# Expert down products two blocks behind, a fourth slot for inner activations, two places for spare blocks, and a second attention turned by DMA

## The chip, the cores and the metric

The kernel runs on one core of one Trainium2 chip. The metric is the time of one execution on the device in microseconds (us). Engines by their short names: PE (TensorE, PEld its weight loads), DVE (VectorE), ACT (ScalarE), POOL (GpSimd), SP (SyncE); SPq, POOLq are the parts of SP and POOL that issue DMAs.

## The reference

Four sequences of 512 tokens, width 512. First a cross attention, then a mixture of eight experts (two per token) beside a shared feed-forward net:

```python
x = x + xattn(layernorm(x), ctx, Wq, bq, Wk, bk)
    # q = ctx Wq^T + bq, k = ctx Wk^T + bk, A = softmax(q k^T)
    # x_m[l, m] = sum_n layernorm(x)[l, n] * A[m, n]
h = layernorm(x)
x = x + moe(h) + (silu(h @ sw_gate) * (h @ sw_up)) @ sw_down * sigmoid(h @ shared_gate_w)
    # moe: softmax over 8 logits, the two largest, made to sum to 1;
    # expert e: (silu(h @ w_gate[e]) * (h @ w_up[e])) @ w_down[e],
    # w_gate, w_up: 512 x 352, w_down: 352 x 512; shared net: 512 x 1408, 1408 x 512
```

## The kernel before, in words

Every large product is made of three products of 16-bit halves (a high and a low part, `PAIRS`), so that each product of two matrices is three matmuls, and whoever makes an operand makes both halves: usually ACT the high one (a cast) and DVE the low one (a subtraction).

**Stage 1, the prologue (0 to about 48 us).** Attention of sequence b=0 and the start of that of b=1, with the order on each engine written out by hand. On DVE: statistics, normalize, five small operations that split the router's weights (`gw3`), then row maxima and scaling of the attention rows in turn.

**Stage 2, the shared net (to about 445 us).** `ffn_block(t)` for t = 0 to 3, 11 tiles j of 128 inner units each: PE does gate(j), up(j) and down(j-2), twelve matmuls each. Between them it does pieces of the attention of b = t+1. Tables (`AT_POINT_FIRST` for t=0, `AT_POINT`, `AT_POINT_LAST`) say at which point (j, "gate"/"up"/"down") which piece stands, and all engines read the same tables, so a piece stands at the same point of each engine's own program. The pieces: `attn`/`attn_lows` (attention rows transposed by PE, halved by ACT and DVE), `attn_high`/`attn_low` with `turn_attention` (rows halved first, then transposed by DMA from SP's queue; used for b = 2 and 3), `mix` (the product with normed x, 48 matmuls), `assign`/`places` (places of tokens in the experts' lists), `stats2`, `norm2`, `halves`. The shared net's weights are loaded and split tile by tile meanwhile, tiles 0 to 3 by POOL.

**Stage 3, the experts (445 us to the end).** Rows were scattered by expert into a scratch tensor `xs_dram`. 39 blocks of 128 rows are worked through: as many as any routing could fill. The reference sends 529, 574, 526, 500, 502, 468, 474 and 523 rows of these inputs to the eight experts, which is 5+5+5+4+4+4+4+5 = 36 real blocks (0 to 35); blocks 36 to 38 are spare, and all their rows lead to padding rows of `out`. For a block k: SP's `load_block` brings x transposed, PE does gate and up (12 matmuls of 352 columns each), ACT `block_silu`, DVE `block_product`, ACT `hidden_high` and DVE `hidden_low` make halves, SP's `turn_hidden` transposes them by DMA into one of three slots, PE does `expert_down` (9 matmuls), ACT `weigh` scales the result into `yblk`, and POOL `add_result` adds it to `out` by an indirect DMA. PE's order is up(k), gate(k+1), down(k-1). Block 38's inner activations are turned by PE itself (`turn_last_hidden`), then halved (`last_hidden_high`, `last_hidden_low`).

Adds of blocks that may hit the same rows must not overlap. Block k always waits for the add of block k-2; it waits for that of block k-1 too, unless `table[3]` says that both have the same expert (whose rows are all different). For spare blocks `same_expert` is 0, so each waits for the one before:

```python
                if k >= 2:
                    pool.wait_ge(y_added[k % 2], 16 * (k // 2))
                ...
                if k >= 1:
                    pool.wait_ge(y_added[(k - 1) % 2], ahead)
```

Of the kernel before, what the change touches and what calls it, by code (L numbers as in the profile page):

```python
# [13 lines left out]
P = 128  # L14
# [89 lines left out]
def build_xattn_moe(nc, x, ctx_in, w_q, b_q, w_k, b_k, gate_w, w_gate, w_up, w_down,  # L104
# [23 lines left out]
    X_SLOTS = 4  # L128
    XF = E + 4
    SPARE = E * NT  # L130
    DUMP = SPARE + (NBLK - MIN_BLK) * P
    META = H
# [38 lines left out]
    with ExitStack() as stack:  # L171
# [12 lines left out]
        def four_banks(b, stage):  # L184
            return first_two(b) and (b == 0 or stage != "logits") and stage != "assign"
# [45 lines left out]

        attn_rows = normed_own.rearrange("p t h -> p (t h)").bitcast(F16).rearrange("p (t n) -> p t n", t=RT)

        class AttentionPlace:

            def __init__(self, ctx_rows, normed, xnT, expo, attn_space):
                self.ctx_rows, self.normed, self.xnT, self.expo = ctx_rows, normed, xnT, expo
                self.attnT = attn_space.rearrange("p (a t n) -> p a t n", a=2, t=RT)

# [16 lines left out]
        def place(b):  # L256
# [6 lines left out]
        hidT = hidden[:, :, :, :].rearrange("p s a n -> p (s a n)")[:, 0:3 * 2 * DC * P].rearrange(  # L263
            "p (s a n) -> p s a n", s=3, a=2)
        hid_rows = hT[:, 1].rearrange("p a c s -> p (a c s)").bitcast(BF16)[:, 0:3 * 2 * DC * P].rearrange(
            "p (s a n) -> p s a n", s=3, a=2)
# [61 lines left out]
        pad_id = sb("pad_id", [P, 1], I32)  # L328
        count = sb("count", [P, E], F32)
# [13 lines left out]
        same_expert = sb("same_expert", [P, NBLK], F32)  # L343
        pad_full = sb("pad_full", [P, E], F32)
# [56 lines left out]
        aT_in = [sem(f"aT_in{b}") for b in range(2, B)]  # L401
# [5 lines left out]
        hid_in = [sem(f"hid_in{i}") for i in range(3)]  # L407
# [20 lines left out]
        def _(sp):  # L428
# [48 lines left out]
            sp.dma_start(place(1).ctx_rows, ctx_in[1].rearrange("(t p) c -> p t c", p=P)).then_inc(ctx1_loaded, 16)  # L477
            load_rows(1, x1_loaded)
# [18 lines left out]
            def turn_attention(b):  # L497

                sp.wait_ge(energy_done, RT * b + RT)
                for i in range(RT):  # L500
                    sp.wait_ge(a_row_low, RT * (b - 2) + i + 1)
                    sp.dma_start(by_tile(place(b).attnT, i), attn_rows[:, i, :],
                                 transpose=True).then_inc(aT_in[b - 2], 16)
# [11 lines left out]
            for j in range(2, 8):  # L515
                load_unit_tile(j)
# [1219 lines left out]
```

## Time and profile before

| | us |
|---|---|
| median of 3 runs (lowest, highest) | 683.58 (683.12, 683.95) |
| the profiled execution's own time | 683.55 |
| its span in the profile | 681.8 |
| PE busy in it | 653.4 (96%) |
| DVE, ACT, POOL busy | 301.3, 229.1, 163.6 |

The profile is of one execution, and its time lies within the runs. A row of the timeline begins with the start and the length in us; in square brackets stands how long the engine had been idle and what ended that. Line numbers are those of the kernel before.

### The profile page before, as it was taken

What the parts mean: (1) busy time and instruction counts of PE and PEld (TensorE: products, weight loads), DVE (VectorE), ACT (ScalarE), POOL (GpSimd) and SP (SyncE); (2) the same over time, 40 slices, a digit from 0 to 9 for tenths busy, and PEclk for the clock granted to TensorE, in tenths of its full rate; (3) what the DMA queues carried; (4) which work ended last, traced back from release to release, by engine and by line L of the source; (5) the groups of instructions that cost most, each with busy time, mean ns of one, the idle gap of its engine ahead of it and who ended that gap; (6) DMA issues with size and microseconds to landing.
All of it is one profiled execution on the core that took longest, in us unless ns stands there. A gap on an engine that the chain in (4) does not pass through costs nothing.

```text
span 681.8 us, 10320 instructions
## 1 busy us (share of the span) xinstructions
PE 653.4 (96%) x3426; PEld 333.1 (49%) x3426; DVE 301.3 (44%) x703; ACT 229.1 (34%) x341; POOL 163.6 (24%) x134
## 2 busy tenths in 40 slices
PE   8889999999999999999999999999999999999990
PEld 5454444444444444444444444455555555555550
DVE  3998574525523445432549874452222222222220
ACT  3445143313620223630434543432222322222320
POOL 2560180004000004100344360013222222222221
PEclk9989999999999999999999999999999999999996
DMA  8531097313430313430167886447879888878962
GB/s 278 186 92 48 1 304 211 114 58 131 95 61 0 57 37 125 125 63 0 31 169 250 309 302 173 141 118 129 131 128 132 132 131 133 135 126 139 131 74 31
DMA packets 146899, 85.77 MB, mean 126 GB/s; under 512 B 109721, under 2 KB 131481, under 8 KB 146850
## 3 DMA queue, kind: packets, MB, share of 16 engines
q1 hardware_dynamic: 134722, 56.25, 35.6%
q0 software_dynamic: 10544, 27.30, 18.2%
q10 hardware_dynamic: 1584, 1.57, 0.7%
q8 instruction: 31, 0.51, 0.3%
q14 instruction: 18, 0.15, 0.1%
HBM read 32.76 MB, written 27.29 MB: 88 GB/s over the span
## 4 chain that ended last, share of the span: by engine, by line
PE 75%; DVE 8%; DMA 8%; SPq 2%; issue 2%; ACT 1%; POOL 1%; POOLq 0%; ACTq 0%
PE bank L1594 27%; PE bank L1642 16%; PE bank L1609 14%; PE bank L1669 9%; PE bank L1451 5%; DMA hidden<-hT 3%; DMA out<-staging,token_blk 2%; DMA staging<-L_ffn_w_gate 2%; PE bank L1408 1%; SPq L531 1%; DMA arena<-x 1%; PE bank L1417 1%; POOL arena L641 1%; DVE arena L1288 1%; DVE stats L936 1%
## 5 line engine op out<-in xcount | busy, mean ns | idle before, releaser
L1594 PE MATMUL bank<-hT,arena 128*128 128x512 f16 x1056 | 237.7, 379 | 0.5 <-DVE prod L1314 0.5
L1594 PEld LDWEIGHTS bank<-hT,arena 128*128 128x128 bf16 x1056 | 102.6, 98 | 126.2 <-issue 4.6
L1642 PE MATMUL bank<-arena,hx_odd 128*128 x936 | 145.9, 313 | 0.0
L1609 PE MATMUL bank<-arena,hidden 128*128 128x512 bf16 x528 | 120.4, 379 | 0.0
L1642 PEld LDWEIGHTS bank<-arena,hx_odd 128*128 128x128 f16 x936 | 90.8, 97 | 54.0 <-issue 0.9
L657 POOL DMA_INDIRECT out<-staging,token_blk x39 | 61.1, 1566 | 163.5 <-ACT staging L913 133.1
L1351 DVE TENSOR_TENSOR prod<-silu_sb,bank 128x352 f32<-128x352 f32 x39 | 20.3, 521 | 149.8 <-PE bank L1642 149.8
L1669 PE MATMUL bank<-arena,hidden 128*128 (+1 forms) x351 | 82.3, 379 | 3.5 <-DMA hidden<-hT 1.7
L1609 PEld LDWEIGHTS bank<-arena,hidden 128*128 128x128 bf16 x528 | 51.3, 98 | 63.1 <-issue 2.3
L1314 DVE TENSOR_TENSOR prod<-silu_sb,bank 128x512 f32<-128x512 f32 x44 | 30.1, 685 | 73.8 <-PE bank L1594 69.7
L875 ACT ACTIVATE silu_sb<-bank 128x512 f32<-128x512 f32 x44 | 26.2, 595 | 104.4 <-PE bank L1594 104.2
L869 ACT CAST hidden<-prod 128x512 bf16<-128x512 f32 x44 | 26.9, 617 | 86.3 <-DVE prod L1314 86.3
L1669 PEld LDWEIGHTS bank<-arena,hidden 128*128 128x128 bf16 (+1 forms) x351 | 34.2, 98 | 41.0 <-issue 6.1
L913 ACT ACTIVATE staging<-bank,w_blk 128x512 f32<-128x512 f32 x39 | 26.8, 687 | 63.8 <-PE bank L1669 63.8
L1319 DVE TENSOR_TENSOR hidden<-prod,hidden 128x512 bf16<-128x512 f32 x44 | 35.0, 799 | 29.1 <-ACT hidden L869 28.9
L609 POOL TENSOR_TENSOR rstd<-var_eps,minus_half 128x4 f32<-128x4 f32 x8 | 9.7, 1207 | 156.5 <-DVE var_eps L949 156.3
L1451 PE MATMUL bank<-arena 128*128 128x512 f16 x192 | 43.1, 379 | 0.0
L901 ACT CAST hT<-prod 128x352 bf16<-128x352 f32 x38 | 18.4, 484 | 63.5 <-DVE prod L1351 63.5
L1288 DVE TENSOR_TENSOR arena<-staging,arena 128x1408 bf16<-128x1408 f32 (+1 forms) x14 | 23.5, 1679 | 14.8 <-ACT arena L845 14.8
L1451 PEld LDWEIGHTS bank<-arena 128*128 128x128 f16 x192 | 18.8, 98 | 23.0 <-issue 0.6
L845 ACT CAST arena<-staging 128x1408 bf16<-128x1408 f32 (+1 forms) x18 | 25.1, 1398 | 13.4 <-DMA staging<-L_ffn_w_gate 9.9
L892 ACT ACTIVATE silu_sb<-bank 128x352 f32<-128x352 f32 x39 | 18.1, 463 | 28.8 <-PE bank L1642 28.8
(190 smaller groups left out, 512.8 us busy)
## 6 DMA issues: line engine op xcount, KB each, us to landing
staging<-L_ffn_w_gate SPq DMA_DIRECT2D x6, 704.0 KB, 5.2
staging<-L_ffn_w_up SPq DMA_DIRECT2D x6, 704.0 KB, 5.9
arena<-x SPq DMA_DIRECT2D x3, 1024.0 KB, 7.4
out<-arena POOLq DMA_DIRECT2D x3, 1024.0 KB, 4.8
staging<-L_ffn_w_down SPq DMA_DIRECT2D x6, 512.0 KB, 4.8
staging<-L_ffn_sw_gate SPq DMA_DIRECT2D x11, 256.0 KB, 3.1
staging<-L_ffn_sw_up SPq DMA_DIRECT2D x11, 256.0 KB, 3.7
staging<-L_ffn_sw_down SPq DMA_DIRECT2D x11, 256.0 KB, 4.6
```

The lines of the kernel that those rows point to most:

```text
L657: nc.gpsimd.indirect_dma_start(out=out[:, :], out_offset=bass.IndirectOffsetOnAxis(ap=token_blk[:, k:k + 1], axis=0), in_=yblk[:, k % 2, : ...
L869: nc.scalar.copy(hidden[:, j % 3, HI, :], prod[:, j % 2, :]).then_inc(hid_hi, 1)
L875: nc.scalar.activation(silu_sb[:, :], gate_ps[:, :], ACT.Silu).then_inc(silu_ready, 1)
L913: nc.scalar.activation(yblk[:, k % 2, :], bank[4 + k % 2][:, :], ACT.Copy, scale=w_blk[:, k:k + 1]).then_inc(y_ready, 1)
L1288: nc.vector.tensor_tensor(arena[:, at + gap:at + gap + n], piece_space[piece_slot(q)][:, 0:n], arena[:, at:at + n], ALU.subtract).then_inc ...
L1314: nc.vector.tensor_tensor(prod[:, j % 2, :], silu_sb[:, :], up_ps[:, :], ALU.mult).then_inc(prod_ready, 1)
L1319: nc.vector.tensor_tensor(hidden[:, j % 3, LO, :], prod[:, j % 2, :], hidden[:, j % 3, HI, :], ALU.subtract).then_inc(hid_lo, 1)
L1451: op = nc.tensor.matmul(att_bank(b, "mix", i)[:, :], place(b).xnT[:, xp, c, i * P:(i + 1) * P], place(b).attnT[:, ap, c, :], start=(c == 0 ...
L1594: op = nc.tensor.matmul(ps[:, :], weights[:, j, wp, kind, c * P:(c + 1) * P], hT[:, t % 2, hp, c, :], start=(c == 0 and s == 0), stop=(c = ...
L1609: op = nc.tensor.matmul(out_ps[i][:, :], hidden[:, j % 3, hp, i * P:(i + 1) * P], weights[:, j, wp, DOWN, :], start=(j == 0 and s == 0), s ...
L1642: op = nc.tensor.matmul(ps[:, 0:I], xT[:, k % X_SLOTS, xp * KC + c, :], arena[:, bass.ds(at + (part_at(0, part) + wp * low_gap(part) + c * ...
L1669: op = nc.tensor.matmul(ps[:, :], hidT[0:n, k % 3, hp, c * P:(c + 1) * P], arena[0:n, bass.ds(at + (DOWN_AT + wp * DN + c * H), H)], start ...
```

## The change

Six edits, all in the order of work or in what waits for what; the results are computed with the same products.

1. PE's order in the expert stage becomes up(k), gate(k+1), down(k-2); inner activations have four slots (`HID_SLOTS`), and ACT's `weigh` follows by one block more. At the end PE transposes the last block's activations inside down(37), ahead of its last three matmuls.
2. Spare blocks go alternately to two sets of padding rows; `same_place` lets a spare block whose predecessor is spare skip the wait for it. Three more small DMAs fill the odd spare blocks' token columns, and one more clears the second padding rows.
3. The attention of b=1 is turned as those of 2 and 3 are: halves by ACT and DVE, four DMA transposes on SP's queue, no PE transposes.
4. `mix` of b=1 and what follows from it stand one tile j later; it uses two banks instead of four, so that down(0) of t=0 no longer waits for it.
5. In the prologue DVE takes row maxima and scaling ahead of the five `gw3` operations, and one row maximum ahead of normalize.
6. SP holds the load of x[1] (and all behind it) until x[0] has landed; POOL splits tile 3 after `h_low` instead of after normalize; SP loads tile 8 ahead of `turn_h(1)`.

```diff
 AT_POINT_FIRST = {
-    (1, "gate"): [("attn_lows", 0)],
-    (1, "up"): [("attn", 0), ("attn", 1), ("attn", 2), ("attn", 3)],
-    (1, "down"): [("assign", 0)],
-    (2, "gate"): [("mix", 0), ("mix", 1), ("mix", 2), ("mix", 3)],
-    (2, "up"): [("stats2", 0)],
+    (1, "gate"): [("attn_high", 0), ("attn_high", 1)],
+    (1, "up"): [("attn_low", 0), ("attn_low", 1), ("attn_high", 2), ("attn_high", 3)],
+    (1, "down"): [("attn_low", 2), ("attn_low", 3), ("assign", 0)],
     (2, "down"): [("halves_before", 0)],
-    (3, "gate"): [("norm2", 0)],
-    (3, "up"): [("halves", 0)],
+    (3, "gate"): [("mix", 0), ("mix", 1), ("mix", 2), ("mix", 3)],
+    (3, "up"): [("stats2", 0)],
+    (4, "gate"): [("norm2", 0)],
+    (4, "up"): [("halves", 0)],
...
+            sp.wait_ge(x0_loaded, 16)
             load_rows(1, x1_loaded)
...
-            for j in range(2, 8):
+            for j in range(2, 6):
+                load_unit_tile(j)
+            turn_attention(1)
+            for j in range(6, 9):
                 load_unit_tile(j)
             turn_h(1)
...
-                if k >= 3:
-                    sp.wait_ge(ed_done, k - 2)
+                if k >= HID_SLOTS:
+                    sp.wait_ge(ed_done, k + 1 - HID_SLOTS)
...
                 for n in range(NBLK - MIN_BLK):
-                    pool.dma_start(xs_dram[SPARE + n * P:SPARE + (n + 1) * P, :],
-                                   pad_row[:, :]).then_inc(spare_filled, 16)
+                    spare = xs_dram[SPARE + n * P:SPARE + (n + 1) * P, :]
+                    if n % 2:
+                        pool.dma_start(spare[:, 0:TOKEN], pad_row[:, 0:TOKEN]).then_inc(spare_filled, 16)
+                        pool.dma_start(spare[:, TOKEN:XW], pad_odd[:, :]).then_inc(spare_filled, 16)
+                    else:
+                        pool.dma_start(spare, pad_row[:, :]).then_inc(spare_filled, 16)
...
-            pool.wait_ge(normed_ready[1], RT)
+            pool.wait_ge(hlo_ready, KC)
             for j in range(3, POOL_TILES):
                 split_unit_tile(j)
...
             for k in range(NBLK - 1):
                 hidden_high(k)
                 block_silu(k + 1)
-                if k > 0:
-                    weigh(k - 1)
+                if k > 1:
+                    weigh(k - 2)
+            weigh(NBLK - 3)
+            last_hidden_high()
             weigh(NBLK - 2)
-            last_hidden_high()
             weigh(NBLK - 1)
...
+                    nc.vector.tensor_tensor(same_place[:, 1:NBLK], same_expert[:, 1:NBLK], ended[:, 0:NBLK - 1, E - 1],
+                                            ALU.add)
...
-                    nc.vector.scalar_tensor_tensor(out=table[:, 3, 1:NBLK], in0=same_expert[:, 1:NBLK], scalar=-16.0,
+                    nc.vector.scalar_tensor_tensor(out=table[:, 3, 1:NBLK], in0=same_place[:, 1:NBLK], scalar=-16.0,
...
+                if i < 2 and b == 1:
+                    pe.wait_ge((logits_read, places_read)[i], b)
+                if i >= 2 and b >= 1:
                     pe.wait_ge(added, RT * b + i - 1)
...
                         if t == 0:
-                            pe.wait_ge(added, RT * b + RT)
+                            pe.wait_ge(exp_done, RT * b + RT)
+                            pe.wait_ge(xlo_ready, KC * b + KC)
...
                     n = chunk(c)
+                    if k == NBLK - 2 and c == DC - 1:
+                        turn_last_hidden()
...
-                if k == 1:
+                if k == 2:
                     pe.wait_ge(piece_low_dve, PIECES - POOL_LOW)
-                if k > 0:
-                    expert_down(k - 1, down_from)
-                down_from = pe.value_load(table[0:1, 2, k:k + 1], min_val=0, max_val=(E - 1) * 2 * DN)
-            turn_last_hidden()
-            expert_down(NBLK - 1, down_from)
+                if k > 1:
+                    expert_down(k - 2, down_from.pop(0))
+                down_from.append(pe.value_load(table[0:1, 2, k:k + 1], min_val=0, max_val=(E - 1) * 2 * DN))
+            expert_down(NBLK - 2, down_from.pop(0))
+            expert_down(NBLK - 1, down_from.pop(0))
```

Where this moves instructions, at three places. First PE in `ffn_block(0)`, before: from up(0), gate(1) and up(1) on (the 36 matmuls of L1594; L1434 is `turn_attn`, L1498 to L1504 `places`, L1451 `mix`, L1609 down):

```order
L1594 MATMUL bank<-hT,arena 128x512 x36
L1434 MATMUL bank<-ident,hx_odd 128x128 x16
L1498 MATMUL bank<-mask,earlier 128x32
L1501 MATMUL bank<-mask,ones 128x24
L1501 MATMUL bank<-mask,ones 128x16
L1501 MATMUL bank<-mask,ones 128x8
L1504 MATMUL bank<-mask,ones 128x8 x4
L1594 MATMUL bank<-hT,arena 128x512 x12
L1451 MATMUL bank<-arena 128x512 x48
L1594 MATMUL bank<-hT,arena 128x512 x12
L1609 MATMUL bank<-arena,hidden 128x512 x12
```

The same place on PE after the change (L1613 gate and up, L1629 down, L1472 `mix`):

```order
L1613 MATMUL bank<-hT,arena 128x512 x36
L1519 MATMUL bank<-mask,earlier 128x32
L1522 MATMUL bank<-mask,ones 128x24
L1522 MATMUL bank<-mask,ones 128x16
L1522 MATMUL bank<-mask,ones 128x8
L1525 MATMUL bank<-mask,ones 128x8 x4
L1613 MATMUL bank<-hT,arena 128x512 x24
L1629 MATMUL bank<-arena,hidden 128x512 x12
L1613 MATMUL bank<-hT,arena 128x512 x12
L1472 MATMUL bank<-arena 128x512 x48
L1613 MATMUL bank<-hT,arena 128x512 x12
```

The 16 transposes are gone, and up(2), down(0) and gate(3), 36 matmuls, now stand ahead of `mix`.

Second, DVE in `ffn_block(0)` after the change, from the last `inverse_sum` of b=1 to the product of tile 2 (L979 `x_low`, L1331 a product, L1027 `attn_row_low`, L1336 `low_part`); before, four `attn_low` stood between `x_low` and the product, and none behind it:

```order
L994 RECIPROCAL inv_sum<-sum_scaled 128x1 [waits sum_ready]
L979 TENSOR_TENSOR arena<-bank,arena 128x512 [waits xhi_ready] x4
L1331 TENSOR_TENSOR prod<-silu_sb,bank 128x512 [waits silu_ready,up_done]
L1027 SCALAR_TENSOR_TENSOR arena<-hx_odd,inv_sum,arena 128x512 [waits a_row_high] x2
L1336 TENSOR_TENSOR hidden<-prod,hidden 128x512 [waits hid_hi] x2
L1027 SCALAR_TENSOR_TENSOR arena<-hx_odd,inv_sum,arena 128x512 [waits a_row_high] x2
```

The last two of these rows release the last two DMA transposes of `turn_attention(1)`.

Third, ACT at the end of the program, before, from `hidden_high` of block 37 on (L901; L892 `block_silu`, L913 `weigh`, L905 `last_hidden_high`):

```order
L901 CAST hT<-prod 128x352 [waits hid_in1,ep_ready]
L892 ACTIVATE silu_sb<-bank 128x352 [waits ep_ready,eg_done]
L913 ACTIVATE staging<-bank,w_blk 128x512 [waits y_added0,meta_ready,ed_done]
L913 ACTIVATE staging<-bank,w_blk 128x512 [waits y_added1,meta_ready,ed_done]
L905 CAST hidden<-bank 128x384 [waits last_turned]
L913 ACTIVATE staging<-bank,w_blk 128x512 [waits y_added0,meta_ready,ed_done]
```

And after (L918, L909, L930 and L922):

```order
L918 CAST hT<-prod 128x352 [waits hid_in1,ep_ready]
L909 ACTIVATE silu_sb<-bank 128x352 [waits ep_ready,eg_done]
L930 ACTIVATE staging<-bank,w_blk 128x512 [waits y_added1,meta_ready,ed_done]
L930 ACTIVATE staging<-bank,w_blk 128x512 [waits y_added0,meta_ready,ed_done]
L922 CAST hidden<-bank 128x384 [waits last_turned]
L930 ACTIVATE staging<-bank,w_blk 128x512 [waits y_added1,meta_ready,ed_done]
L930 ACTIVATE staging<-bank,w_blk 128x512 [waits y_added0,meta_ready,ed_done]
```

Behind the last silu four blocks are still to be weighed, 35 to 38, where there were three.

## Rows read from the trace of the kernel before

**Rows 1.** Stretches: length, busy us (instructions) of PE, PEld, DVE, ACT, POOL; PEclk, DMA share, GB/s.

```profile
45.00:48.00 3.00, 3.00 (x16) 2.98 (x15) 2.93 (x7) 1.92 (x5) 2.35 (x2) 0.50 0.51 146
68.00:85.00 17.00, 17.00 (x81) 7.67 (x79) 8.99 (x23) 3.12 (x4) 2.12 (x1) 1.00 0.00 1
```

**Rows 2.** Timeline, PE in `ffn_block(0)` around the second attention.

```profile
51.95 7.93 PE L1594 MATMUL bank<-hT,arena 128*128 128x512 f16 x36
60.97 2.36 PE L1434 MATMUL bank<-ident,hx_odd 128*128 128x128 f32 x16 [1.09 <-DVE arena L961]
...
65.95 10.52 PE L1451 MATMUL bank<-arena 128*128 128x512 f16 x48
76.31 2.75 PE L1594 MATMUL bank<-hT,arena 128*128 128x512 f16 x12
```

**Rows 3.** Timeline, PE in the expert stage: first products, first down, block 38's up.

```profile
445.22 9.11 PE L1642 MATMUL bank<-arena,hx_odd 128*128 x60
455.20 2.12 PE L1669 MATMUL bank<-arena,hidden 128*128 x9 [0.86 <-DMA hidden<-hT]
...
658.17 1.96 PE L1642 MATMUL bank<-arena,hx_odd 128*128 x12
```

**Rows 4.** Chain that ended last, two points four blocks apart: start, us, what.

```profile
513.72 3.58 PE bank L1642 x24
...
535.83 3.59 PE bank L1642 x24
```

**Rows 5.** Timeline, the end: adds of blocks 35, 36, 38, `weigh` of 36 and 38.

```profile
653.99 1.55 POOL L657 DMA_INDIRECT out<-staging,token_blk  x1 [4.15 <-ACT staging L913]
...
658.37 0.69 ACT L913 ACTIVATE staging<-bank,w_blk 128x512 f32<-128x512 f32 x1 [1.48 <-PE bank L1669]
659.33 1.56 POOL L657 DMA_INDIRECT out<-staging,token_blk  x1 [3.79 <-ACT staging L913]
...
666.05 0.69 ACT L913 ACTIVATE staging<-bank,w_blk 128x512 f32<-128x512 f32 x1 [2.89 <-PE bank L1669]
670.34 1.56 POOL L657 DMA_INDIRECT out<-staging,token_blk  x1 [3.88 <-DMA out<-staging,token_blk]
```

**Rows 6.** Timeline, DVE in `ffn_block(0)`: last inverse, `x_low`, two `low_part`.

```profile
59.35 0.15 DVE L973 TENSOR_SCALAR sum_scaled<-exp_sum 128x1 f32<-128x1 f32 x1
...
60.13 2.48 DVE L961 TENSOR_TENSOR arena<-bank,arena 128x512 f16<-128x512 f32 x4
...
65.52 1.46 DVE L1319 TENSOR_TENSOR hidden<-prod,hidden 128x512 bf16<-128x512 f32 x2
```

**Rows 7.** b=2's `attn_row_low` (timeline), and line L502's DMA transposes (ns; to landing).

```profile
185.36 1.41 DVE L1009 SCALAR_TENSOR_TENSOR arena<-arena,inv_sum 128x512 f16<-128x512 f32 x2
...
L502 SPq DMA_TRANSPOSE arena<-arena x8: 1232/1282/1338, 186.2 to 296.2; - x8
DMA to landing us min/median/max: 3.1/3.2/3.4
```

**Rows 8.** Timeline, prologue: energies of b=0, DVE's order, the product that waits.

```profile
13.79 3.60 PE L1417 MATMUL bank<-arena 128*128 128x512 f32 x8
14.70 1.92 DVE L955 TENSOR_SCALAR arena<-arena,mean_var,rstd 128x512 f32<-128x512 f32 x4 [1.17 <-POOL rstd L609]
...
17.53 1.28 DVE L966 TENSOR_REDUCE neg_max<-bank 128x1 f32<-128x512 f32 x2
...
22.61 0.68 DVE L961 TENSOR_TENSOR arena<-bank,arena 128x512 f16<-128x512 f32 x1
23.27 1.88 PE L1408 MATMUL bank<-arena 128*128 128x512 f32 x4
```

**Rows 9.** The adds of line L657 as a group: time to landing after issue.

```profile
DMA to landing us min/median/max: 4.6/4.8/6.8
```

**Rows 10.** Timeline, PE's idle time ahead of the slow stretch.

```profile
44.19 3.00 PE L1461 MATMUL bank<-ident,arena 128*128 128x128 f32 x16 [2.62 <-DVE arena L955]
```

**Rows 11.** Timeline, the issue of `turn_h(1)`'s four DMA transposes on SP.

```profile
96.62 11.29 SPq L512 DMA_TRANSPOSE hT<-hx_odd  x4
```

More of the change, by code:

```diff
@@ L128, in build_xattn_moe @@
     X_SLOTS = 4
+    HID_SLOTS = 4
     XF = E + 4
@@ L184, in four_banks @@
         def four_banks(b, stage):
-            return first_two(b) and (b == 0 or stage != "logits") and stage != "assign"
+            return first_two(b) and (b == 0 or stage not in ("logits", "mix")) and stage != "assign"
         def att_bank(b, stage, i):
@@ L400, in build_xattn_moe @@
         xT_in = [sem(f"xT_in{b}") for b in range(2, B)]
-        aT_in = [sem(f"aT_in{b}") for b in range(2, B)]
+        aT_in = [sem(f"aT_in{b}") for b in range(1, B)]
         hT_in = [sem(f"hT_in{b}") for b in range(1, B)]
@@ L406, in build_xattn_moe @@
         hid_pad, hid_row_high, hid_row_low = sem("hid_pad"), sem("hid_row_high"), sem("hid_row_low")
-        hid_in = [sem(f"hid_in{i}") for i in range(3)]
+        hid_in = [sem(f"hid_in{i}") for i in range(HID_SLOTS)]
         last_turned, last_high, last_low = sem("last_turned"), sem("last_high"), sem("last_low")
@@ L513, in turn_h @@
                                  transpose=True).then_inc(hT_in[b - 1], 16)
-            for j in range(2, 8):
+            for j in range(2, 6):
+                load_unit_tile(j)
+            turn_attention(1)
+            for j in range(6, 9):
                 load_unit_tile(j)
             turn_h(1)
-            for j in range(8, UT):
+            for j in range(9, UT):
                 load_unit_tile(j)
@@ L677, in _ @@
             fill_spare()
-            pool.dma_start(out[NT:NT + P, :], pad_row[:, 0:H]).then_inc(spare_filled, 16)
+            for n in range(2):
+                pool.dma_start(out[NT + n * P:NT + (n + 1) * P, :], pad_row[:, 0:H]).then_inc(spare_filled, 16)
             send_rows(0)
@@ L742, in attn_row_high @@
                 act.wait_ge(inv_ready, RT * b + n + 1)
-                if n == 0:
+                if n == 0 and b >= 2:
                     act.wait_ge(x_row_low, b - 1)
-                nc.scalar.activation(attn_rows[:, n, 0:S], place(b).expo[:, n, :], ACT.Copy,
+                elif n == 0:
+                    act.wait_ge(x_turned, KC * b + KC)
+                nc.scalar.activation(place(b).attn_rows[:, n, 0:S], place(b).expo[:, n, :], ACT.Copy,
                                      scale=inv_sum[:, n:n + 1]).then_inc(a_row_high, 1)
@@ L1181, in _ @@
             statistics(0, 0)
+            row_max(0, 0)
             normalize(0, 0)
+            row_max(0, 1)
+            scale_attn(0, 0)
+            row_max(0, 2)
+            scale_attn(0, 1)
+            row_max(0, 3)
+            scale_attn(0, 2)
+            x_low(0, 0)
             gw_ps = bank[7][:, 0:KC * NL].rearrange("p (k e) -> p k e", k=KC)
@@ L1253, in attention @@
                         attn_row_low(b, i)
-                    elif stage == "attn_lows":
-                        for c in range(KC):
-                            attn_low(b, c)
                     elif stage == "mix":
@@ L1563, in attention @@
                         energy(b, i)
-                    elif stage == "attn":
-                        turn_attn(b, i)
                     elif stage == "mix":
@@ L1725 @@
     n_tokens, n_experts = shape[0] * shape[1], inputs["L0_ffn_w_gate"].shape[0]
-    out = nc.dram_tensor("out", (n_tokens + P, shape[2]), F32, kind="ExternalOutput").ap()
+    out = nc.dram_tensor("out", (n_tokens + 2 * P, shape[2]), F32, kind="ExternalOutput").ap()
     xs_rows = n_experts * n_tokens + (n_experts - 1) * P + n_experts * P
```

97 lines of the change are left out of this document (47 added, 50 removed).

## The prediction

> **What bounds the kernel now.** I read the stretches first: PE is busy for all of 68 to 85 us at full clock [rows 1], and of the whole span 96% (the table). So only two kinds of time can be won: PE's own waits and work, and what follows PE's last matmul. I then followed PE alone for its waits, and the chain of waits for the end. Three places matter here.
>
> In the shared net PE waits 1.09 us ahead of the second attention's transposes and then spends 2.36 us on them [rows 2]; up(1) ended at 51.95 + 7.93 = 59.88, `mix` begins at 65.95 and takes 76.31 - 65.95 = 10.36 for 48 matmuls, so 2.59 for a group of twelve.
>
> In the expert stage an undisturbed block takes (535.83 - 513.72) / 4 = 5.53 us, 3.58 of it gate and up, 1.95 down [rows 4]. From the first product at 445.22 to block 38's up at 658.17 lie 212.95 us [rows 3]. They hold 77 half products (39 gates, 38 ups) and 37 downs, which is 36 x 5.53 + 5 x 1.79 + 1.95 = 210.0. So PE lost 3.0 us, and a row shows how: the first down waited 0.86 us idle for the DMA that transposes inner activations (`hidden<-hT`).
>
> At the end PE is not the bound. Block 38's `weigh` is over at 666.05 + 0.69 = 666.74, its add starts at 670.34, after a wait for a DMA: the add before it [rows 5]. The adds of 35, 36 and 38 start at 653.99, 659.33 and 670.34, so one waiting for the other costs 5.34, then 11.01 / 2 = 5.5 each.
>
> **Second attention.** Removed from PE: the wait and the transposes. I assume that gate(0) starts when it did (prologue, below). Then up(1) ends at 59.88, `places` takes at most some 0.4 (estimate: between 60.97 and the next gate, at 65.95 - 2.59 = 63.36, all but 0.03 us is the transposes, so it mostly overlaps), and gate(2), up(2), down(0), gate(3) run from 60.3 to 70.7. Will the operands be there? On DVE: inverse from 59.35, about 0.35; `x_low` 2.48 [rows 6] to 62.2; the product of tile 1, of `low_part`'s shape, 0.7, to 62.9, in time for up(2) at 62.9; two `attn_row_low` 1.4 [rows 7]; two `low_part` 1.46 to 65.7, the first of them in time for down(0) at 65.5; two more `attn_row_low` to 67.1. ACT's four casts run ahead of these, and its silu and halves have the 2.59 us of each PE group. SP issues the third transpose at 66.4 and the fourth at about 67.75; each takes 1.28 to issue and lands 3.2 later [rows 7]: 72.25. So `mix` starts at 72.35 and PE waits 1.65 us: a new stall in place of the old one. Up(2), down(0) and gate(3) (7.77 us) have moved ahead of it, so the start that compares with 65.95 is 72.35 - 7.77 = 64.6, whatever `places` takes. **Gain 1.4.** Bounds: with transposes that land by 70.7 it is 3.0; with the slowest landing of the row, 3.4, 1.2. What follows is one tile later, with 7.77 us per tile to cover it. `mix` in two banks makes its third part wait for the add of the first, which has the 2.59 us of the second part for its 0.7. SP's queue: tile 6 stands behind the transposes but waits for tile 4's split anyway, in tile 2's up; tile 8 is loaded ahead of `turn_h(1)`, which needs 11.3 us of SP and leaves 20 to the logits in tile 8.
>
> **Prologue.** DVE works nearly without a break from 14.70 on. Normalize started there; now the row maximum goes first, and the first energy is done at 13.79 + 3.60 / 4 + latency, about 14.85. The order behind it is the same work in another sequence. The `gw3` operations (16.6 to 17.5 [rows 8]) now come after the third scaling and one `x_low`; PE's project(1,1), which overwrites their bank and started at 23.27, waits for them. Summed, DVE reaches their end at 14.85 + 0.64 + 1.83 (to normalize's end) + 5.5 (three row maxima, scalings and `x_low`) + 1.0 = 23.8 at most, 23.2 if its present wait for ACT goes. I take nothing; bounds -0.6 and +0.3, since DVE is the chain there. Holding x[1] costs nothing by these rows: statistics of b=1 come after all this.
>
> **Down two behind.** The transpose of block k now has one more block, 5.53 us, to land in; the waits were a fraction of a microsecond each. SP's work per block does not grow, and the fourth slot keeps its wait for `ed_done` at a block long done. Adds, `yblk` slots and silu keep their distance to PE. **Gain 3.0**, bounds 2.0 (if a third of the loss is not the transposes') and 3.0.
>
> **The end.** Down(35) moves behind gate(38), where down(36) stood, so `weigh`(35) starts where that of 36 did (658.37) with one down less ahead of it: 1.95 earlier, and with the gains above. An add starts 1.0 after its `weigh` does (block 36) [rows 5]. Block 36 is spare but 35 is not, so 36 still waits for 35: +5.34. 37 has no wait for 36 any more. 38 goes to the same rows as 36 and waits for it: +5.5. In all 658.37 - 1.95 + 1.0 + 5.34 + 5.5 = 668.3 before the gains above, against 670.34: **gain 2.0**. So three of the four adds still follow each other; the change takes one landing out of the chain but puts one block more behind PE's last gate. Block 38's `weigh`, 666.74 less 4.4 = 662.3 even if the moved transposes win nothing, is ready before its add may start (668.3 - 4.4 = 663.9), so that move is hidden by 1.6 us. Bounds: an add's landing lies between 4.6 and 6.8 [rows 9]; if 37, issued meanwhile, delays 36's landing to the slowest, the gain is 0; if 35's add starts earlier than I think, 2.5.
>
> The four more DMAs on POOL stand ahead of its first row scatter, in the shared net; they delay that by four issues, and what waits for the scatter (ACT's halving of x for b=2, SP's first block load) comes tiles later. Nothing; without that cover, four issues.
>
> **Sum.** 1.4 + 3.0 + 2.0 = 6.4. The profiled execution took 683.55, next to the median 683.58: 683.55 - 6.4 = **677.1**.
>
> **Rivals.**
> - The clock. PE ran at 1.2 GHz from 45 to 48 (granted 0.50 [rows 1]), after 2.62 us without work [rows 10]. If the new wait before `mix` does the same, three microseconds at half rate cost 1.5: 678.6. Against it: the wait is shorter, between full groups, and the present wait of 1.09 was not followed by a fall (1.00 in 68 to 85). The Trainium skill ("TensorE: Matmul & The Clock Gate", "Why this matters for your kernels") warns of idle gaps between bursts of matmuls for just this reason; the trace agrees at 45 us and shows no fall for a short gap.
> - The stalls stay: the transposes were late by little, and something else (PE's own instruction supply) sets part of the loss. Two of the three microseconds stay: 679.1. For it: only 0.86 of the loss is a row here. Against: that row names the DMA.
> - The end gains nothing, as two adds in flight share the DMA engines and land late: 679.1.
> - Slower: the four transposes of the second attention issue as those of `turn_h(1)` did, 11.29 us for four [rows 11]. From 63.6 that ends at 74.9, lands at 78.1, PE waits 7.4 instead of 1.65, and after such a wait the clock falls, 1.5 more: 677.1 + 5.75 + 1.5 = 684.4. It decides from a landing past about 77.2 on (5.0 later, with the fall). Against: `turn_h(1)` ran beside POOL's row scatters, while in 68 to 85 the DMA engines are idle (share 0.00). The Trainium skill ("DMA: Bandwidth & Descriptors", "Issuing engines are not separate DMA queues") says that DMAs of all engines run on the same 16 and interleave; by that rule it is the other traffic that counts, and the row shows none here.
>
> **How the numbers follow.** Forecast 0.58; clock 0.12; stalls stay 0.10; end gains nothing 0.13; slower 0.05; nothing measurable 0.02 (several bounds at once). The range goes from 674.8 (transposes in time 1.6, end 0.5, prologue 0.3, taken from 677.1) to 680.6 (the end's and the clock's rivals together, 2.0 + 1.5): about 0.85. A measurement of this kernel can tell some 0.2% (1.4 us) from no change: faster 0.91, same 0.04, slower 0.05.
>
> **What would show it.** After: no PE transposes of the second attention, one wait of about 1.7 us before `mix` in tile 3; no wait for `hidden<-hT` in the expert stage, whose first product to block 38's up takes about 208 us (one down less); the last four adds with 36 some 5.3 after 35, 37 within 2 to 3 of 36, 38 some 5.5 after 36. The prediction is wrong if DVE's chain before 60 us moved by over half a microsecond, if the wait before `mix` exceeds 3, or if the add of 38 waits for its `weigh`.

## The result, and the profile after

The changed kernel took 676.0 us in the median of 4 runs (674.98 to 676.14); the kernel before 683.77 beside it. The ratio is 0.9885, with a 95% interval of 0.9868 to 0.9902: faster by 7.8 us, where 6.4 were forecast (677.1). The profiled execution is the fastest of the four, 674.98, with a span of 673.3.

From the two traces the 683.55 - 674.98 = 8.57 us between the profiled executions fall to these stretches. They are cut where one piece of work starts that both kernels have: gate(0) of the shared net, the first product of the expert stage, the adds of blocks 35 and 38.

| stretch | before | after | gain | forecast |
|---|---|---|---|---|
| start to gate(0) | 48.56 | 46.41 | 2.15 | 0 |
| gate(0) to first expert product | 396.66 | 394.10 | 2.56 | 1.4 |
| first expert product to add of 35 | 208.77 | 209.26 | -0.49 | -0.4 |
| add of 35 to add of 38 | 16.35 | 11.65 | 4.70 | 5.5 |
| add of 38 to the end | 13.21 | 13.56 | -0.35 | 0 |

(The forecast's terms "down" and "end", 3.0 and 2.0, are laid out by this table's cuts: its add of 35 was 658.37 - 1.95 + 1.0 - 3.0 = 654.42, against 653.99 before, and its adds took 5.34 + 5.5.)

The second attention, timeline of PE, what answers to [rows 2]: gate(2), up(2), down(0), gate(3), then `mix`.

```profile
57.77 2.75 PE L1613 MATMUL bank<-hT,arena 128*128 128x512 f16 x12
60.78 2.76 PE L1613 MATMUL bank<-hT,arena 128*128 128x512 f16 x12 [0.26 <-DVE prod L1331]
63.38 2.75 PE L1629 MATMUL bank<-arena,hidden 128*128 128x512 bf16 x12
65.97 2.75 PE L1613 MATMUL bank<-hT,arena 128*128 128x512 f16 x12
68.91 10.52 PE L1472 MATMUL bank<-arena 128*128 128x512 f16 x48 [0.18 <-issue]
```

Its four DMA transposes on SP (timeline), and DVE's last pair of low halves ahead of them:

```profile
61.47 5.46 SPq L508 DMA_TRANSPOSE arena<-arena  x4
```

```profile
63.17 1.41 DVE L1027 SCALAR_TENSOR_TENSOR arena<-hx_odd,inv_sum,arena 128x512 f16<-128x512 f32 x2
```

No transposes stand on PE any more, and the wait ahead of `mix` is 0.18 where 1.65 was forecast. Less the three groups that moved ahead (7.77), `mix` starts at 61.14, that is 14.73 after gate(0); before it was 65.95 - 48.56 = 17.39.

The stretches of [rows 1] and the prologue, after (windows, then timeline of PE; [rows 8, 10] before):

```profile
45.00:48.00 3.00, 2.71 (x19) 1.67 (x18) 2.42 (x5) 2.99 (x6) 0.00 (x0) 1.00 0.12 44
68.00:85.00 17.00, 16.82 (x79) 7.46 (x78) 8.97 (x13) 3.62 (x4) 0.00 (x0) 1.00 0.17 49
```

```profile
13.00 3.60 PE L1434 MATMUL bank<-arena 128*128 128x512 f32 x8
...
22.38 1.98 PE L1425 MATMUL bank<-arena 128*128 128x512 f32 x4 [0.92 <-DVE gw L1223]
...
43.22 2.02 PE L1482 MATMUL bank<-ident,arena 128*128 128x128 f32 x16 [2.45 <-DVE arena L973]
```

The energies start 0.79 earlier, and the sixteen transposes near 44 us take 2.02 instead of 3.00: in this execution the granted clock stayed at 1.00 (2.4 GHz), though the idle time ahead of them, 2.45, is nearly that of before, 2.62. The eight transposes behind them are faster too, so from the start of the sixteen to gate(0) lie 3.19 instead of 4.37. These two, 0.79 and 1.18, make 2.0 of the 2.15. The experiments show that both come and go from run to run.

The expert stage (timeline of PE, [rows 3] before), and the down products as a group of the page:

```profile
440.51 12.69 PE L1662 MATMUL bank<-arena,hx_odd 128*128 x84
453.04 2.11 PE L1691 MATMUL bank<-arena,hidden 128*128 x9
...
648.42 1.96 PE L1662 MATMUL bank<-arena,hx_odd 128*128 x12
```

```profile
L1691 PE MATMUL bank<-arena,hidden 128*128 (+1 forms) x351 | 82.2, 379 | 0.6 <-DVE hidden L1378 0.6
```

No down product waits for a DMA now; the stage takes 648.42 - 440.51 = 207.91 (forecast 208).

The end (timeline of POOL and ACT, [rows 5] before): adds of 35 to 38 and `weigh` of 38.

```profile
649.77 1.55 POOL L673 DMA_INDIRECT out<-staging,token_blk  x1 [4.16 <-ACT staging L930]
655.11 1.55 POOL L673 DMA_INDIRECT out<-staging,token_blk  x1 [3.78 <-DMA out<-staging,token_blk]
656.96 1.56 POOL L673 DMA_INDIRECT out<-staging,token_blk  x1 [0.30 <-issue]
661.42 1.55 POOL L673 DMA_INDIRECT out<-staging,token_blk  x1 [2.91 <-ACT staging L930]
```

```profile
659.77 0.69 ACT L930 ACTIVATE staging<-bank,w_blk 128x512 f32<-128x512 f32 x1 [4.45 <-DMA out<-staging,token_blk]
```

36 follows 35 by 5.34, as forecast, and 37 follows 36 by 1.85, a little under the 2 to 3 forecast; 38 follows 36 by 6.31, not 5.5. The row of `weigh` shows a wait that the prediction overlooked (it took the slots of `yblk` to keep their distance): weighed rows have two slots, so 38's slot is free only when the add of 36 has landed. In this trace the add of 38 waits for that `weigh`, which the prediction had named as a sign that it is wrong; experiment 10 tests what the wait cost.

### The profile page after: what moved, and what is told of

It is laid out like the page before. It is cut to its first block, busy times and chain, and to the rows that moved or that the text cites. A ratio compares the mean times of both kernels' runs of the same rounds, so it can differ in the third digit from the quotient of the medians.

```text
span 673.3 us, 10294 instructions
## 1 busy us (share of the span) xinstructions
PE 648.0 (96%) x3410; PEld 329.6 (49%) x3410; DVE 300.0 (45%) x700; ACT 229.3 (34%) x341; POOL 161.7 (24%) x139
## 4 chain that ended last, share of the span: by engine, by line
PE 76%; DVE 8%; DMA 5%; issue 5%; ACT 2%; POOL 1%; POOLq 0%; SPq 0%; ACTq 0%; DVEq 0%
PE bank L1613 27%; PE bank L1662 17%; PE bank L1629 14%; PE bank L1691 9%; PE bank L1472 5%; DMA out<-staging,token_blk 3%; PE bank L1425 2%; DMA staging<-L_ffn_w_gate 2%; PE bank L1434 1%; POOL arena L657 1%; DVE arena L1305 1%; DVE neg_max L984 1%; DMA arena<-L_xattn_Wk 1%; DVE arena L973 1%; DVE prod L1331 1%
## 5 line engine op out<-in xcount | busy, mean ns | idle before, releaser
L1613 PE MATMUL bank<-hT,arena 128*128 128x512 f16 x1056 | 237.8, 379 | 1.2 <-DVE prod L1331 0.9
L1613 PEld LDWEIGHTS bank<-hT,arena 128*128 128x128 bf16 x1056 | 102.5, 98 | 127.1 <-issue 5.1
L1629 PE MATMUL bank<-arena,hidden 128*128 128x512 bf16 x528 | 120.3, 379 | 0.0
L1629 PEld LDWEIGHTS bank<-arena,hidden 128*128 128x128 bf16 x528 | 51.4, 98 | 63.0 <-issue 2.3
L892 ACT ACTIVATE silu_sb<-bank 128x512 f32<-128x512 f32 x44 | 26.2, 595 | 102.1 <-PE bank L1613 102.0
L1331 DVE TENSOR_TENSOR prod<-silu_sb,bank 128x512 f32<-128x512 f32 x44 | 30.1, 683 | 67.7 <-PE bank L1613 63.6
L930 ACT ACTIVATE staging<-bank,w_blk 128x512 f32<-128x512 f32 x39 | 26.8, 687 | 61.0 <-PE bank L1691 56.6
L1336 DVE TENSOR_TENSOR hidden<-prod,hidden 128x512 bf16<-128x512 f32 x44 | 34.9, 798 | 28.4 <-ACT hidden L886 28.3
L1472 PE MATMUL bank<-arena 128*128 128x512 f16 x192 | 43.1, 379 | 0.2 <-issue 0.2
L918 ACT CAST hT<-prod 128x352 bf16<-128x352 f32 x38 | 18.4, 485 | 63.7 <-DVE prod L1368 63.7
L1472 PEld LDWEIGHTS bank<-arena 128*128 128x128 f16 x192 | 18.7, 98 | 23.4 <-issue 1.2
L909 ACT ACTIVATE silu_sb<-bank 128x352 f32<-128x352 f32 x39 | 18.1, 463 | 28.8 <-PE bank L1662 28.8
```

Source lines behind the costliest of these rows:

```text
L892: nc.scalar.activation(silu_sb[:, :], gate_ps[:, :], ACT.Silu).then_inc(silu_ready, 1)
L930: nc.scalar.activation(yblk[:, k % 2, :], bank[4 + k % 2][:, :], ACT.Copy, scale=w_blk[:, k:k + 1]).then_inc(y_ready, 1)
L1331: nc.vector.tensor_tensor(prod[:, j % 2, :], silu_sb[:, :], up_ps[:, :], ALU.mult).then_inc(prod_ready, 1)
L1336: nc.vector.tensor_tensor(hidden[:, j % 3, LO, :], prod[:, j % 2, :], hidden[:, j % 3, HI, :], ALU.subtract).then_inc(hid_lo, 1)
L1472: op = nc.tensor.matmul(att_bank(b, "mix", i)[:, :], place(b).xnT[:, xp, c, i * P:(i + 1) * P], place(b).attnT[:, ap, c, :], start=(c == 0 ...
L1613: op = nc.tensor.matmul(ps[:, :], weights[:, j, wp, kind, c * P:(c + 1) * P], hT[:, t % 2, hp, c, :], start=(c == 0 and s == 0), stop=(c = ...
```

## The experiments

All times are medians of 5 to 12 runs. The three sets, run beside the kernel before, had medians of 685.13, 684.86 and 684.74 for it; the changed kernel once more had 675.57. The kernel before varies from set to set, so the ratio to it says more than the time, and differences of under about 1.4 say little.

**1. Without the hold.**

```diff
-            sp.wait_ge(x0_loaded, 16)
             load_rows(1, x1_loaded)
```

> The changed kernel (676.0) with one part of edit 6 undone: SP no longer holds the load of x[1] until x[0] has landed. Theory: the hold is what makes the prologue 0.8 to 1.0 shorter, because the first projection's operands share the DMA engines with x[1] no longer (its eight to nine microseconds fell by 0.78). Then this run is at 676.8 to 677.0, the first projection takes about 8.9 again, the energies of b=0 start at about 13.8 and not 13.0. Rival: the prologue's gain is the new order of DVE (edit 5); then 676.0 and the energies at 13.0.

676.39 (676.08 to 677.86; ratio to before 0.988, 0.9862 to 0.9898). The energies stayed at 13.0 (timeline of PE):

```profile
13.03 3.60 PE L1433 MATMUL bank<-arena 128*128 128x512 f32 x8
...
43.26 3.48 PE L1481 MATMUL bank<-ident,arena 128*128 128x128 f32 x16 [2.46 <-DVE arena L972]
```

So the hold does not make the first stretch shorter, and the theory is out. The second row shows the stretch at half clock again, behind an idle time like that of the kernel after.

**2. The old order of DVE in the prologue.** Normalize first, then the five `gw3` operations, then row maxima and scalings, as before.

```diff
-            row_max(0, 0)
             normalize(0, 0)
-            row_max(0, 1)
-            scale_attn(0, 0)
...
+            row_max(0, 0)
+            row_max(0, 1)
+            scale_attn(0, 0)
...
```

> The changed kernel (676.0) with edit 5 undone: DVE normalizes, splits the router's weights, and only then takes row maxima and scalings of b=0. Theory: the order is the same work in another sequence and is worth 0.1 to 0.2 at most: 676.1 to 676.2, with the second product of b=1's projection (22.38 after, 23.27 before) within 0.3 of 22.4. Rival: the order is what moved PE by 0.9 there; then 676.9 to 677.0 and that product at about 23.3.

675.95 (674.6 to 681.01; ratio 0.9878, 0.9849 to 0.9906); energies at 12.94, the product in question at 22.37. The order is worth nothing that these runs can tell, as the theory had it; the rival is out.

**3. Spare blocks wait as before.** Two sets of padding rows, but the old rule.

```diff
-nc.vector.scalar_tensor_tensor(out=table[:, 3, 1:NBLK], in0=same_place[:, 1:NBLK], scalar=-16.0,
+nc.vector.scalar_tensor_tensor(out=table[:, 3, 1:NBLK], in0=same_expert[:, 1:NBLK], scalar=-16.0,
```

> The changed kernel (676.0) with the rule of edit 2 undone: spare blocks still have two sets of padding rows, but each spare block waits for the add ahead of it, as before the change. Theory: the end is bound by adds that wait for landings, so 36 follows 35 by 5.3, 37 follows 36 by 5.4 and 38 follows 37 by 5.4; the add of 38 then stands 16.1 behind that of 35 and not 11.65 as after, so 4.5 is lost: 680.5. Rival: adds that overlap land later, so the saving is partly taken back: 678 to 679; or the last product ends so late that the waits cost nothing: 676.0.

680.43 (679.04 to 682.23; ratio 0.9933, 0.9914 to 0.9952). The adds of 35 to 38 (timeline of POOL):

```profile
650.21 1.55 POOL L673 DMA_INDIRECT out<-staging,token_blk  x1 [4.16 <-ACT staging L930]
655.85 1.55 POOL L673 DMA_INDIRECT out<-staging,token_blk  x1 [4.09 <-DMA out<-staging,token_blk]
661.43 1.55 POOL L673 DMA_INDIRECT out<-staging,token_blk  x1 [4.03 <-ACT staging L930]
667.02 1.55 POOL L673 DMA_INDIRECT out<-staging,token_blk  x1 [4.03 <-DMA out<-staging,token_blk]
```

16.81 from 35 to 38 instead of 11.65 (the theory had 16.1), and 4.4 more in the medians (4.5): the theory holds, and this is the biggest single term of the change. `weigh` of 37 (timeline of ACT), released by the landing of 35:

```profile
655.18 0.69 ACT L930 ACTIVATE staging<-bank,w_blk 128x512 f32<-128x512 f32 x1 [0.28 <-DMA out<-staging,token_blk]
```

**4. The experts' edits alone**, 1 and 2, on the kernel before.

> The kernel before (683.8) with edits 1 and 2 alone: down products two behind, four slots, two sets of padding rows; attention, prologue and loads as before. Theory: the parts add up, so this gives 3.05 in the expert stage and 1.2 at the end: 679.5, and the first product of the expert stage stands at about 445.2 as before. Rival: part of the end's or of the stage's gain comes from the earlier start (loads of the experts' weights in another order), then 680.5 or more; or the shared net's edits gave nothing but a different clock, then 676 to 678.

680.19 (678.0 to 680.59; ratio 0.9921, 0.9903 to 0.9939), against 685.13 beside it: 4.9 less, where the theory had 4.25 from a kernel before of 683.8. First product at 445.17, add of 35 209.26 behind it, as in the kernel after; 38 stands 12.15 behind 35. The two edits work without the others.

**5. The second attention alone**, edits 3 and 4 with the loads' place, on the kernel before.

> The kernel before (683.8) with edits 3 and 4 alone, and the place of the loads of tiles 6 to 8 in SP's queue that goes with them; prologue's order, hold and experts as before. Theory: the second attention is worth 2.7 (no wait and no transposes on PE), and the prologue's 0.8 does not belong to it: 681.1, the energies of b=0 at 13.8. Rival: the shorter first transposes on PE (0.66 and 1.04 against 1.12 and 1.42) come with this edit, since neither the hold nor the order of DVE brought them: then 680.3 and the energies at 13.0.

682.81 (681.32 to 684.69; ratio 0.9971, 0.9955 to 0.9987), against 684.86 beside it: 2.05. From gate(0) (48.30) to the first product (441.70) lie 393.40, which is 3.3 less than before; but in the profiled run 36 follows 35 by 6.31 and not 5.34, which takes 1.0 back. The energies stand at 13.88, so the slow first transposes are there with this edit as well; since they come and go (experiment 9), one trace does not settle the rival. In this trace the time gained in the shared net reaches the end less what the landings of the last adds took.

**6. Down products one block behind again**, with four slots.

```diff
...
-                if k > 1:
-                    expert_down(k - 2, down_from.pop(0))
+                if k > 0:
+                    expert_down(k - 1, down_from.pop(0))
...
-            expert_down(NBLK - 2, down_from.pop(0))
```

> The changed kernel (676.0) with the order of edit 1 undone: PE's down products and ACT's weighing follow one block behind again, with four slots and with the last transposes inside down(37). Theory: the chain of the last four adds starts at the add of 35, and that add gains nothing from edit 1: the stage is 3 longer, but down(35) stands one block earlier, so the add of 35 starts at 440.51 + 212.95 - 4.18 = 649.3 instead of 649.77, and 36, 37 and 38 follow it as after: 675.5 to 676.2, with the waits for the DMA transposes back on PE. Rival: the terms add up as I summed them, so the stage's 3.0 is lost: 679.0.

678.87 (676.98 to 681.39; ratio 0.9912, 0.9885 to 0.9939): my theory fell, and edit 1 is worth 2.9 in the medians. The waits of PE for inner activations from the first product on (us in total, times, longest), here and, in the second fence, in the kernel before:

```profile
PE bank L1690 <- DMA hidden<-hT: 3.8, 7, 1.1
```

```profile
PE bank L1669 <- DMA hidden<-hT: 1.7, 4, 0.9
```

I had taken the stage's 212.95 from one trace of before. Here the waits are seven, not four, the stage takes 659.24 - 444.19 = 215.05, and the add of 35 stands 210.87 behind the first product (208.77 before, 209.26 after). That is 1.6 later than after. The adds of 35 to 38 take 12.58 - 11.65 = 0.9 more, since here the end hangs on PE's last down product, for which `weigh(38)` waits (timeline of ACT):

```profile
666.68 0.69 ACT L930 ACTIVATE staging<-bank,w_blk 128x512 f32<-128x512 f32 x1 [2.03 <-PE bank L1690]
```

So in the traces the order is worth 1.6 + 0.9 = 2.5. This profiled run (680.93) is slow for other reasons too: half clock near 44 us, and a stall in the shared net behind the late loads on SP's queue (last section), timeline of PE:

```profile
127.02 5.35 PE L1612 MATMUL bank<-hT,arena 128*128 128x512 f16 x24 [1.37 <-DVE arena L1310]
```

How many of the six runs had this stall is not known, so the 2.9 of the medians may hold some of it.

**7. Three slots instead of four.**

```diff
-    HID_SLOTS = 4
+    HID_SLOTS = 3
```

> The changed kernel (676.0) with three slots for inner activations instead of four; all else the same. Theory: the fourth slot is not needed, since the slot of block k is free when down(k-3) is done, which PE has ahead of up(k): 676.0, no wait for inner activations on PE. Rival: with down two behind, three slots hold back the DMA transposes: 1 to 3 more, 677 to 679.

676.39 (675.84 to 677.72; ratio 0.9875, 0.9853 to 0.9897). No wait for inner activations in the trace either. The fourth slot is not needed: the order alone does it.

**8. `mix` at its old place.**

```diff
+    (2, "gate"): [("mix", 0), ("mix", 1), ("mix", 2), ("mix", 3)],
+    (2, "up"): [("stats2", 0)],
     (2, "down"): [("halves_before", 0)],
-    (3, "gate"): [("mix", 0), ("mix", 1), ("mix", 2), ("mix", 3)],
-    (3, "up"): [("stats2", 0)],
-    (4, "gate"): [("norm2", 0)],
-    (4, "up"): [("halves", 0)],
+    (3, "gate"): [("norm2", 0)],
+    (3, "up"): [("halves", 0)],
```

> The changed kernel (676.0) with edit 4's place undone: mix of b=1 and what follows from it stand one tile j earlier, as before the change, while its operand still comes by DMA transposes. Theory: the last transpose lands at about 68.8 whatever PE does, mix would be reached at 60.4, so PE waits some 8 us ahead of it, nearly all of the 7.8 that covered it, and the granted clock falls after such a wait for 1.2 more: 684 to 685. Rival: without tile 2's product and halves between them, DVE and ACT give their halves earlier and the last transpose lands by 65: the wait is 4 to 5 and the time 680 to 681.

686.35 (684.27 to 687.32; ratio 1.0018, 1.0004 to 1.0032): no faster than the kernel before, 684.86 beside it. Timeline of PE and SP, then windows:

```profile
59.65 2.75 PE L1613 MATMUL bank<-hT,arena 128*128 128x512 f16 x12
70.57 12.98 PE L1472 MATMUL bank<-arena 128*128 128x512 f16 x48 [8.17 <-issue]
```

```profile
63.15 5.47 SPq L508 DMA_TRANSPOSE arena<-arena  x4
```

```profile
67.00:70.00 3.00, 0.00 (x0) 0.00 (x0) 0.69 (x6) 0.00 (x0) 0.00 (x0) 0.50 0.95 182
70.00:73.00 3.00, 2.43 (x6) 0.87 (x7) 0.00 (x0) 0.00 (x0) 0.00 (x0) 0.50 0.00 0
73.00:76.00 3.00, 3.00 (x9) 1.08 (x8) 0.19 (x1) 0.00 (x0) 0.00 (x0) 0.57 0.00 0
```

The transposes issue and land as in the kernel after, so PE waits 8.17 us. Behind the wait the granted clock is 0.50 (1.2 GHz) until about 75 us, and `mix` takes 12.98 instead of 10.52: 2.5 more, twice the 1.2 that I expected. Edit 3 without the later place of `mix` is a loss: edits 1 and 2 alone took 680.19. The Trainium skill ("TensorE: Matmul & The Clock Gate", "Why this matters for your kernels") warns of just such idle gaps; this trace agrees, at 2.5 us for one.

**9. The changed kernel again.**

> The changed kernel once more, beside the three that follow. Theory: 676.0 in the median. The profiles so far put PE's first transposes at 287 ns each in five runs and at 435 in five, and a stretch at half clock near 45 or 21 us in eight of ten, without regard to the edit; so single times between 674.9 and 677.5 and a profile that may have either. Rival: these two go with the edits and the changed kernel has neither: all times near 675.

675.57 (674.72 to 676.85; ratio 0.9867, 0.9845 to 0.9889). Its profile has the fast first transposes (energies at 13.28) and no fall (2.03 for the sixteen), 11.61 from 35 to 38. Timeline of PE:

```profile
13.28 3.60 PE L1434 MATMUL bank<-arena 128*128 128x512 f32 x8
...
43.74 2.03 PE L1482 MATMUL bank<-ident,arena 128*128 128x128 f32 x16 [2.45 <-DVE arena L973]
```

**10. Four slots for weighed rows.** `yblk` gets four, `weigh(k)` waits for the add of k-4.

```diff
...
-                if k >= 2:
-                    act.wait_ge(y_added[k % 2], 16 * (k // 2))
+                if k >= 4:
+                    act.wait_ge(y_added[k % 2], 16 * (k // 2 - 1))
```

> The changed kernel (676.0) with four slots for the weighed rows that wait for their add, instead of two: weigh(38) no longer waits for the landing of the add of 36. Theory: this wait is the term that the forecast of the end left out; the add of 38 then follows the landing of 36 at once, at about 5.0 behind its start and not 6.3: 1.3 less, 674.7. Rival: the add of 38 is held by the landing of 36 in any case, and weighing after it was a matter of 0.5: 675.5; or nothing, 676.0.

676.49 (675.5 to 676.57; ratio 0.9873, 0.9853 to 0.9893). `weigh(38)` and the adds of 36 to 38 (timeline of ACT, of POOL):

```profile
658.67 0.69 ACT L930 ACTIVATE staging<-bank,w_blk 128x512 f32<-128x512 f32 x1 [2.03 <-PE bank L1691]
```

```profile
656.59 1.55 POOL L673 DMA_INDIRECT out<-staging,token_blk  x1 [3.94 <-DMA out<-staging,token_blk]
658.44 1.56 POOL L673 DMA_INDIRECT out<-staging,token_blk  x1 [0.30 <-issue]
663.03 1.55 POOL L673 DMA_INDIRECT out<-staging,token_blk  x1 [3.04 <-DMA out<-staging,token_blk]
```

`weigh(38)` waits for PE alone and is over at 659.36; it starts 2.08 behind the add of 36 and not 4.77 as in experiment 9, yet 38 is added 6.44 behind 36. The wait that I had overlooked was real, and cost nothing: the theory is out.

**11. The first spare block on the second set of padding rows.**

```diff
...
-                    if n % 2:
+                    if n % 2 == 0:
...
-nc.vector.tensor_tensor(same_place[:, 1:NBLK], same_expert[:, 1:NBLK], ended[:, 0:NBLK - 1, E - 1],
+nc.vector.tensor_tensor(same_place[:, 1:NBLK], same_expert[:, 1:NBLK], ended[:, 1:NBLK, E - 1],
```

> The changed kernel (676.0) with the first spare block on the second set of padding rows, so that 36 shares no row with 35 and need not wait for it; 37 goes to the first set, 38 to the second again. Theory: 36 then starts when it is weighed, 3.7 behind 35 instead of 5.3; weigh(38) and the add of 38 still follow the landing of 36: 1.6 to 2.1 less, 674.2. Rival: adds in flight together land later, and the saving is eaten by the landing of 36: 675.5 or more.

673.77 (672.23 to 674.72; ratio 0.9829, 0.9808 to 0.985), 1.8 under experiment 9: as expected, and the fastest of all. The adds:

```profile
651.35 1.55 POOL L673 DMA_INDIRECT out<-staging,token_blk  x1 [4.16 <-ACT staging L930]
654.90 1.55 POOL L673 DMA_INDIRECT out<-staging,token_blk  x1 [2.00 <-ACT staging L930]
657.41 1.55 POOL L673 DMA_INDIRECT out<-staging,token_blk  x1 [0.96 <-ACT staging L930]
661.21 1.55 POOL L673 DMA_INDIRECT out<-staging,token_blk  x1 [2.25 <-ACT staging L930]
```

Only 38 still follows a landing (36's, 6.31 behind it); 35 to 38 takes 9.86.

**12. Both together (10 and 11).**

> Both of the two before this one: four slots for weighed rows, and the first spare block on the second set of padding rows. Theory: the end is then bound by PE's last down product: weigh(38) 2.15 behind its start and the add 1.15 later, 2.9 less than the changed kernel: 673.1, a version faster than both. Rival: the landing of 36 still comes last, since three adds are in flight: 674 to 675.

676.1 (674.59 to 676.97; ratio 0.9865, 0.9843 to 0.9886): theory and rival both missed, this is not the best version. The end is shorter in the trace (9.32 from 35 to 38), but PE stood still in the shared net (timeline of SP, DVE, PE):

```profile
96.37 20.77 SPq L518 DMA_TRANSPOSE hT<-hx_odd  x4
```

```profile
126.15 1.76 DVE L1311 TENSOR_TENSOR arena<-staging,arena 128x1536 bf16<-128x1536 f32 x1 [10.69 <-ACT arena L869]
```

```profile
127.97 5.35 PE L1613 MATMUL bank<-hT,arena 128*128 128x512 f16 x24 [2.07 <-DVE arena L1311]
```

The loads of the tiles behind `turn_h(1)` in SP's queue came so late that DVE's split of a tile held PE for 2.07. One profile shows it; whether most of this kernel's runs had it is open.

## Why the prediction was right, point by point

**Prologue, 0.** The edits are worth nothing that was shown, as forecast: without the hold of edit 6 the time was 676.4, without edit 5 it was 676.0. They were not undone together. In traces with the fall near 44 us, gate(0) starts 34.77 after the energies before, and 34.54 to 34.97 after, in the eight experiments that had both that prologue, or nearly, and the fall (1, 2, 6 to 8, 10 to 12). The 2.0 us that the profiled execution won here is of another kind. PE's first transposes ran at 287 ns each in some executions and at 435 in others (0.66 and 1.12 us for four), and kernels with the new prologue are on both sides: 0.66 after and in experiments 1 to 3 and 9, 1.11 or 1.12 in 7, 8, 11 and 12, between them in 6 and 10. The fall of the clock missed three of eleven (after, 3, 9). All three traces with the old prologue (before, 4, 5) had the slow transposes and a fall; whether edits 5 and 6 change the odds stays open. The clock rival (678.6) did not come: the wait before `mix` was 0.34 at most in the traces with edits 3 and 4 whole, and the granted clock behind it stayed at 1.00; only the 8.17 of experiment 8 brought a fall there.

**Second attention, 1.4.** The mechanism held (no transposes on PE, three groups moved ahead, DVE's halves and SP's four issues where I put them), and the gain was 2.56, inside the bounds of 1.2 and 3.0. The stretch took 393.3 to 394.9 in the other eight traces that have these edits whole and no stall, and 396.36 in experiment 4, which has none of them. The mis-sized step is "each takes 1.28 to issue and lands 3.2 later": the 3.2 of that row counts from the start of the issue. From 61.47 + 5.46 = 66.93, the end of the last issue, to `mix` lie 1.98, and 1.28 + 1.98 is 3.3. I had added 3.2 behind the issue, and so put 1.3 too much into the wait before `mix`. The rival that the transposes issue slowly did not come: 5.46 for four.

**Down two behind, 3.0.** 207.91 against the forecast 208.0, no wait left, so the rival "stalls stay" is out. Before, nearly all of the lost 3.0 lay at six down products: the first waited 0.86, and five more started 5.79 to 6.05 behind the one ahead of them instead of 5.53, which is 1.9 in sum; after, all follow by 5.53 up to the end's. Experiment 6 puts the order's worth at 2.5 in the traces, with all else as after. But the table shows what the two terms, apart, hid: the shorter stage does not make the add of 35 earlier (-0.49), since down(35) moved one block back. By the traces the 3.0 become time only because edit 2 shortens the chain of adds that follows. With edit 1 and the old rule (experiment 3) the first product lies 209.26 + 16.81 = 226.07 ahead of the add of 38, against 225.12 before; with edit 2 and the old order (experiment 6) it is 210.87 + 12.58 = 223.45, and with both 220.91. No run has edit 1 alone. The prediction's sum had this in it, in the term for the end.

**The end, 2.0.** 36 waits for 35, 37 for nobody, 38 for 36: right in kind. The mis-sized step is "38 waits for it: +5.5": 6.31 after, 6.13 in experiment 9. It is neither the slot of `weigh` (experiment 10) nor a late landing: `weigh(38)` is released by the landing of 36 4.66 behind its start, near the least of [rows 9] (4.6), and POOL starts 38 only 1.65 later. Where an add waits for the one just before, experiment 3 has 0.7 to 0.8 for that (`weigh(37)` at 655.18, the add of 36 at 655.85). What I think, and no run here has shown: `add_result` waits first for block k-2 and only then loads `ahead` from the table. For 38 the landing is that first wait, so the load lies behind it; for 36 it lies ahead. Moving the load up would tell.

**The sum.** 8.57 in the profiles, of which 2.0 comes and goes, 7.8 in the medians, 6.4 forecast: the attention's 1.2 above its term, the end's 0.8 and the tail's 0.35 below, and 2.15 from the start. The mechanisms were right; that terms too small and too large partly cancel is luck (without the 2.0 of the start the profiled gain would be 6.6). Two of the three signs that the prediction had named for being wrong came: DVE's chain moved (the sixteen transposes, which it releases, start at 43.22 and not 44.19), for the most part because the energies were 0.79 earlier, and the add of 38 waited for its `weigh`, at no cost. The third, a wait of more than 3 before `mix`, did not. In the later sets the gain was 684.74 - 675.57 = 9.2; experiments 4 and 5 together give 4.9 + 2.1 = 7.0. Whether the rest is scatter or belongs to edits 5 and 6 is open.

## What to carry to other kernels

When a stage is shortened, ask which piece of work starts the last chain, and whether that piece itself moved back: by these traces edit 1's 3 us were worth nothing without edit 2. Where blocks of padding must not meet, choose their places against the last real block too, not only against each other: that one choice gave 1.8 us more. A landing time is read together with the point from which it counts.

## What the runs showed of the hardware that was not expected

The same idle time on PE (2.45 and 2.46 us) was followed by granted clock 1.00 in the kernel after and by sixteen transposes of 3.48 us in experiment 1 (granted 0.50 from 43 to 46 us). The Trainium skill ("TensorE: Matmul & The Clock Gate", "Part 1: The HAM clock gate") says that the warm-up at a kernel's start differs from run to run; these rows show the like for a fall in the middle of a kernel. The granted clock of the first 10 us reads 1.00 in all traces, also where the first transposes took 435 ns.

Four DMA transposes of one shape took 10.2 to 20.9 us of SP's queue, and 11.29 before [rows 11]:

```profile
94.72 19.17 SPq L518 DMA_TRANSPOSE hT<-hx_odd  x4
```

This is `turn_h(1)` in the kernel after. The prediction gave it 11.3 and looked only at the logits behind it; the loads of the tiles behind it are what comes late. At 20.8 and 20.9 (experiments 12 and 6) PE lost 2.07 and 1.37; at 19.5 and less it lost nothing. All runs with the attention's edits but experiment 8 (13.2) had 15.5 or more, the two without them 10.2 and 11.3; which part of the edits does it was not tried.
